# Token shift of the local layers by DMA instead of a matmul, and unit five's up product behind the query and key transposes

## The reference

```
def shift_token(t):                      # half of the channels come from the token before
    t1, t2 = jnp.split(t, 2, axis=-1)
    t2 = jnp.pad(t2, ((0, 0), (1, 0), (0, 0)))[:, :-1]
    return jnp.concatenate([t1, t2], axis=-1)

def _layer(x, wqkv, qs, ksc, wo, lg, lb, w1, b1, w2, b2):
    q, k, v = heads(shift_token(x) @ wqkv)          # 8 heads of 64
    q, k = rotary_xpos(l2norm(q) * qs, l2norm(k) * ksc)
    x = x + local_attention(q, k, v) @ wo           # window 128, causal
    h = shift_token(x)
    h = (h - mean(h)) / sqrt(var(h) + 1e-05) * lg + lb
    a, g = jnp.split(h @ w1 + b1, 2, axis=-1)       # 682 hidden channels each
    return x + (a * gelu(g)) @ w2 + b2
```

## Time and profile before

| | us |
|---|---|
| median of 3 runs | 1770.78 |
| lowest, highest | 1770.05, 1774.5 |
| the profiled execution | 1777.05 |
| its span from the first to the last instruction | 1775.2 |
| phase L1f in the profile | about 486 to 1168 |

### The profile page before, as it was taken

The page is one execution under the profiler, slowest core; times in us unless marked ns, Lnnn a source line. Parts: engine busy times, 40 slices in busy tenths (PEclk is TensorE's granted clock), DMA queues, the critical chain, the costliest instruction groups (busy, mean ns, idle before and its releaser), DMA issues. The chain is left out here.

```text
span 1775.2 us, 38479 instructions
## 1 busy us (share of the span) xinstructions
PE 1678.3 (95%) x11947; PEld 1314.3 (74%) x11992; DVE 1134.9 (64%) x3349; ACT 984.9 (55%) x2789; POOL 936.7 (53%) x1137
## 2 busy tenths in 40 slices
PE   7999799989789999999999999989998999989998
PEld 4788478858646777777777777768876888867886
DVE  4787666638656666766667666547886353336875
ACT  4677345534334566665666656547772355526775
POOL 2366575535456555555555555333677144456752
PEclk9999899999999999999999999999998999999999
DMA  4333276565020000000000000012435244432200
GB/s 156 93 102 119 92 233 196 163 208 180 22 103 1 2 1 1 1 1 1 1 1 1 1 1 1 1 49 83 152 139 184 85 130 143 139 125 76 75 27 25
DMA packets 75574, 138.20 MB, mean 78 GB/s; under 512 B 11697, under 2 KB 57009, under 8 KB 73201
## 3 DMA queue, kind: packets, MB, share of 16 engines
q1 hardware_dynamic: 61648, 96.14, 17.3%
q0 software_dynamic: 13728, 39.60, 6.4%
HBM read 84.88 MB, written 50.82 MB: 76 GB/s over the span
## 5 line engine op out<-in xcount | busy, mean ns | idle before, releaser
L1534 POOL TENSOR_TENSOR L1f_rn<-L1f_ss,L1f_root_c 128x8 f32<-128x8 f32 x64 | 105.6, 1650 | 202.8 <-DVE L1f_ss L1840 200.8
L1667 PE MATMUL L1f_psQ<-L1f_xT,arena 128*128 128x128 f32 x1408 | 167.7, 275 | 0.9 <-ACT L1f_xT L1748 0.9
L1667 PEld LDWEIGHTS L1f_psQ<-L1f_xT,arena 128*128 128x128 f32 x1408 | 164.8, 192 | 2.8 <-ACT L1f_xT L1748 1.1
L2065 POOL DMA_INDIRECT outs_L2f<-L2f_tiles_ys,L2f_tiles_spot x79 | 75.8, 959 | 120.8 <-ACT L2f_tiles_ys L2210 110.5
L1766 ACT ACTIVATE L1f_sg<-L1f_psQ,vec1f 128x128 f32<-128x128 f32 x192 | 63.5, 364 | 118.4 <-PE L1f_psQ L1667 117.6
L1549 POOL TENSOR_TENSOR L1f_rot<-L1f_qn,L1f_sinT 128x512 f32<-128x512 f32 x64 | 113.2, 1788 | 28.8 <-DVE L1f_qn L1856 28.8
L1594 PE MATMUL L1f_psQ<-arena,L1f_hT 128*128 128x512 f32 x256 | 118.4, 605 | 0.6 <-ACT L1f_hT L1755 0.6
L1886 DVE SCALAR_TENSOR_TENSOR L1f_hid<-L1f_psQ,vec1f,L1f_sg 128x128 f32<-128x128 f32 x192 | 61.4, 346 | 78.8 <-ACT L1f_sg L1766 77.7
L2065 POOL DMA_INDIRECT outs_L0f<-L0f_tiles_ys,L0f_tiles_spot x79 | 75.7, 958 | 48.7 <-ACT L0f_tiles_ys L2210 43.0
L1679 PE MATMUL L1f_psB<-arena,L1f_hid 128*128 128x256 f32 (+1 forms) x384 | 99.8, 388 | 0.0
L1539 POOL TENSOR_TENSOR L1f_pr<-L1f_pr,L1f_rs 128x512 f32<-128x512 f32 x64 | 95.6, 1514 | 6.8 <-DVE L1f_rs L1850 6.8
(11 more groups left out here) (534 smaller groups left out, 4682.4 us busy)
## 6 DMA issues: line engine op xcount, KB each, us to landing
L0f_tiles_xs<-rows_L0f SPq DMA_DIRECT2D x79, 144.0 KB, 2.3
L2f_tiles_xs<-rows_L2f SPq DMA_DIRECT2D x79, 144.0 KB, 2.2
arena<-in_w_L2f SPq DMA_DIRECT2D x8, 1120.0 KB, 5.6
arena<-in_w_L1f SPq DMA_DIRECT2D x8, 1088.0 KB, 7.5
L1x_got<-outs_L0f SPq DMA_DIRECT2D x16, 512.0 KB, 3.6
L3x_got<-outs_L2f SPq DMA_DIRECT2D x16, 512.0 KB, 3.4
arena<-in_w_L0f SPq DMA_DIRECT2D x8, 768.0 KB, 4.7
rows_L0f<-zero SPq DMA_DIRECT2D x31, 144.0 KB
```

The costliest lines, as they stand in the source:

```text
L1534: nc.gpsimd.tensor_tensor(rn[:, s.p, h], ss[:, s.p, h], root_c[:, 0:LH], ALU.pow).then_inc(s_rn, 1)
L1667: mm = nc.tensor.matmul(out, w, xT[:, k], start=(k == 0), stop=(k == KC - 1), skip_group_check=True)
L2065: nc.gpsimd.indirect_dma_start(r.outs, bass.IndirectOffsetOnAxis(spot[:, t % YR:t % YR + 1], 0), ys[:, t % YR], None).then_inc(r.s_out[t % ...
```

## The change

The second token shift leaves PE. SP copies partitions 0 to 126 of the upper 128 channels of `Y` to partitions 1 to 127 of a new SBUF tile `ysh`, two buffers by parity of the step; partition 0 keeps the zero of a memset on POOL. DVE waits for the copy on one semaphore per parity and reads `ysh` where it read `psA`. On PE, unit five of `hidden(s, 2)` becomes a piece of its own, `hidden(s, 3)`, behind `turn`. ACT's and DVE's lists keep their order.

```diff
+        ysh = ph.sb("ysh", [P, 2, P])
...
+        s_sh = [ph.sem(f"shifted{i}") for i in range(2)]
...
+            def shift(s):
+                if s.n == 0:
+                    sp.wait_ge(s_one, 4)
+                sp.wait_ge(s_x, s.n + 1)
+                after(sp, s_ln, 2 * s.n - 2)
+                sp.dma_start(ysh[1:P, s.p], Y[0:P - 1, own(s), P:D]).then_inc(s_sh[s.p], 16)
             rounds([(weights_in, 0)])
+            rounds([(shift, -2)])
...
+            nc.gpsimd.memset(ysh[:, :, :], 0.0).then_inc(s_one, 1)
...
             def hidden(s, j):
...
-                for i in range(2):
-                    if j == 2:
+                for i in (0, 1) if j < 2 else (j - 2,):
+                    if j > 1:
                         pe.wait_ge(s_act, U * s.n + 2 + 2 * i)
...
-            def shift(s):
-                pe.wait_ge(s_x, s.n + 1)
-                after(pe, s_xT, s.n)
-                pe.wait_ge(s_hT, min(s.n + 4, N))
-                nc.tensor.matmul(psA[:, 0:P], c.shift, Y[:, own(s), P:D], start=True, stop=True, skip_group_check=True).then_inc(s_sh, 1)
...
-                    (turn_in, 1), (output, -2), (at(hidden, 0), -3), (at(hidden, 1), -3), (at(down, 0), -3), (shift, -2),
-                    (at(hidden, 2), -3), (turn, 0), (at(down, 1), -3), (at(down, 2), -3)])
+                    (turn_in, 1), (output, -2), (at(hidden, 0), -3), (at(hidden, 1), -3), (at(down, 0), -3),
+                    (at(hidden, 2), -3), (turn, 0), (at(hidden, 3), -3), (at(down, 1), -3), (at(down, 2), -3)])
...
             def shifted(s):
-                dve.wait_ge(s_sh, s.n + 1)
-                nc.vector.bn_stats(st[:, s.p, 6:12], psA[:, 0:P]).then_inc(s_st, 1)
+                dve.wait_ge(s_sh[s.p], 16 * (s.n // 2) + 16)
+                nc.vector.bn_stats(st[:, s.p, 6:12], ysh[:, s.p]).then_inc(s_st, 1)
...
-                for k, src in enumerate((Y[:, own(s), 0:P], psA[:, 0:P])):
+                for k, src in enumerate((Y[:, own(s), 0:P], ysh[:, s.p])):
```

More of the change, by code:

```diff
@@ L1489, in local_layers @@
         (s_one, s_mv0, s_root0, s_tab, s_y, s_T, s_hT, s_qk, s_sq, s_ss, s_rn, s_qn, s_cos, s_rot, s_qr, s_qkT, s_qT, s_kT,
-         s_v, s_vx, s_S, s_mx, s_exp, s_rs, s_scaled, s_pt, s_pT0, s_pT1, s_pv, s_oT, s_out, s_x, s_st, s_sh, s_mvf, s_rf,
+         s_v, s_vx, s_S, s_mx, s_exp, s_rs, s_scaled, s_pt, s_pT0, s_pT1, s_pv, s_oT, s_out, s_x, s_st, s_mvf, s_rf,
          s_ln, s_TF, s_xT, s_yb, s_h, s_sg, s_act, s_o, s_res, s_done, s_sm) = ph.semaphores(
             "ones mv0 root0 tab y T hT qk sq ss rn qn cos rot qr qkT qT kT v vx S mx exp rs scaled pt pT0 pT1 pv oT out x "
-            "st shifted mvf rf ln TF xT yb hidden sg act o res done sm")
+            "st mvf rf ln TF xT yb hidden sg act o res done sm")
+        s_sh = [ph.sem(f"shifted{i}") for i in range(2)]
         block = ph.block()
@@ L1515, in _ @@
             nc.gpsimd.memset(spark[:, :], 0.0).then_inc(s_one, 1)
-            pool.wait_ge(s_one, 3)
+            nc.gpsimd.memset(ysh[:, :, :], 0.0).then_inc(s_one, 1)
+            pool.wait_ge(s_one, 4)
             def row_roots(s):
@@ L1651, in turn_in, with unit @@
                 mm.then_inc(s_T, 1)
+            def unit(j, i):
+                return 2 * min(j, 2) + i
             def hidden(s, j):
@@ L1659, in hidden @@
                     after(pe, s_act, U * s.n)
-                for i in range(2):
-                    if j == 2:
+                for i in (0, 1) if j < 2 else (j - 2,):
+                    if j > 1:
                         pe.wait_ge(s_act, U * s.n + 2 + 2 * i)
-                    for m in range(1 if 2 * j + i == U - 1 else 2):
-                        out = unit_out(2 * j + i, m)
+                    for m in range(1 if unit(j, i) == U - 1 else 2):
+                        out = unit_out(unit(j, i), m)
                         for k in range(KC):
-                            w = part(s, UNITS_AT + (2 * j + i) * UNIT_GLU + (m * KC + k) * P, P)
+                            w = part(s, UNITS_AT + unit(j, i) * UNIT_GLU + (m * KC + k) * P, P)
                             mm = nc.tensor.matmul(out, w, xT[:, k], start=(k == 0), stop=(k == KC - 1), skip_group_check=True)
-                    if i == 1 or j == 2:
+                    if i == 1 or j > 1:
                         mm.then_inc(s_h, 1)
```

## The result

| | kernel before | changed kernel |
|---|---|---|
| median, us | 1770.87 (6 runs) | 1762.66 (6 runs) |
| lowest, highest | 1769.8, 1774.5 | 1758.69, 1763.54 |
| span of the profiled execution | 1775.2 | 1760.6 |
| phase L1f in it | 680.94 | 673.76 |
| full round | 20.191 | 19.967 |

The ratio is 0.9948, 95% interval [0.9935, 0.996]: 8.2 us less, where 6.8 were forecast, and the interval reaches from 7.1 to 11.5. The phase's length is from the first to the last start of a PE matmul into its tiles.

A forecast was written before the change was run, and what follows sets the result against it. PE's instruction list was taken to bound full rounds. Removing 31 shifts of 0.22 us gave -6.8 us, the move and copy nothing: 1770.78 - 6.8 = 1764.0 us, own range 1762 to 1766, wider range 1761 to 1774.

The forecast's parts named there:

- What bounds: Full rounds: PE's instruction list sets the length, busy 563.82 of 565.40 us; other engines' waits count only if PE meets them.
- The removed product: Shift matmul on PE: 0.22 us each, 31 of 32 shifts count, 6.8 us less if nothing else gets late.
- The move costs nothing: Unit five behind the transposes: no PE wait becomes late; closest is the key copy, 0.2 us to spare.
- What the move avoids: Unit five in its old place would wait for DVE's products of units two and three, about 0.1 us a round.
- The copy at the high end: SP's copy of 127 partitions, packets one behind another: 4.9 us to land, at no cost to PE.
- The pace of 0.024: Copy on one DMA engine: 0.024 us a packet, from 397 packets in 0.6 us on 16 engines.
- The edge: Copy landing later than 5.5 us after release delays PE at `down`; margin 0.6 us at the high end.
- the late rival: Slower copy packets make `down` wait for DVE's unit four; gain gone from 0.031 us a packet, 1786 us at 0.035; chance 0.16.
- Small parts: Memset of `ysh` on POOL and DVE reading SBUF cost nothing; third round's PE idle grows from 1.01 to over 2 us.
- A second stretch at half clock: Third round, after longer PE idle ahead of the transposes: could cost up to 1.7 us; none taken in the sum.
- More than forecast: Rival: the tail, where hidden layers wait for `normed`, gains a little from earlier statistics; 1762 us, chance 0.04.

The follow-up runs named there:

- e3: Changed kernel without its copy, DVE reading the memset's zeros; full round 19.967 us, ratio to the kernel before 0.9969.
- e4: Changed kernel with the copy split into 112 and 15 partitions; full round 19.967 us, ratio to the kernel before 0.9975.
- e5: Changed kernel with the copy widened to 160, 192 or 256 channels; full rounds 19.967, 20.406, 21.700 us; ratios to the kernel before 0.9968, 1.0061, 1.0426.
- e10: Kernel before with 17 in place of 12 constant matmuls in the third round; third round 20.16 us, ratio to the kernel before 1.0003.
- e11: Changed kernel run once more on another chip; third round 21.55 us, ratio to the kernel before 0.9957.
- e1: Changed kernel with the copy, but unit five back ahead of the transposes; full round 20.146 us, ratio to the kernel before 0.9993.

## Why the prediction was right

- **What bounds.** PE's list sets the round: confirmed by e3 and e4, by e5 with 160 channels, where DVE is 0.9 us late and the round unchanged, and by the same 1.6 us of idle time before and after.
- **The removed product, 0.22 x 31 = 6.8.** Measured 0.224 a round. Of the phase's 7.18 us, 6.28 are the 28 full rounds, 1.83 the third round, of which about 1.6 is the clock, and the tail gives 0.91 back, since its stretch at half clock costs 1.4. The clock's part nearly cancels. The right term is 7.0 (31 x 0.224), as profiles with the stretch in the same place show: e10 against the changed kernel, both in the tail, 680.71 - 673.76 = 6.95, and the kernel before against e11, both in the third round, 680.94 - 674.02 = 6.92. The 0.004 a round above the shift's own time is not located.
- **The move costs nothing.** Right: the key copy ends at 797.59, 0.35 ahead of PE's 797.94, where 0.2 was worked out, because the GELU starts 0.04 after unit five's last matmul ends and not 0.10. Unit five's hidden part is ready at 796.88 for the load at 797.31.
- **What the move avoids, about 0.1 a round.** Undersized: 0.18. That made the second half of the change worth 5 us, as e1's rounds show, and not 3; with this wait most of the gain would have been lost. The sum did not hold this term, so the forecast's number did not test it.
- **The copy at the high end, 4.9 us.** Right in kind, a little long: 4.57, since the first packet and the landing together take 1.5 us. The pace of 0.024 came out right, with some luck: it was read from loads on all engines together, and nothing in that trace showed that one engine copying within SBUF keeps it. The edge is at 5.8 and not 5.5, so the spare time was 1.3 us and not 0.6; by the forecast's own formula the late rival's break-even was nearer 0.034 us a packet than 0.031.
- **Small parts.** The memset took 0.31 us of POOL and moved nothing: the phase's first 54.3 us are the same. A second stretch at half clock, kept for the range, did not come in the changed kernel; the one there was changed its place.
- **More than forecast.** 1762.66 lies nearest this rival's 1762, but not by its mechanism: with the clock alike, the tail gains 39.45 - 39.01 = 0.44 (kernel before and e11), which is two shifts of 0.22 and part of the forecast's 31.
- **The rest.** The measured 8.2 us against the phase's 7.2 is within the intervals (e11's whole ratio is worth 7.8), and nothing shows the 1.0 between them to be the change's; that e3 and e4, with the same rounds, came out at 0.9969 and 0.9975 says how far a median moves by itself. The profiled spans differ by 14.6, of which 7.2 lie in this phase; the other 7.4 lie in phases that the change does not touch. Their stretches at half clock fall differently in every execution, 44.9 us in the profile before and 25.6 in the one after, and 19.3 us less of them can give back up to 9.7. No single pair of profiles should be read for a gain of this size.

## What to carry to other kernels

When one engine is full, taking 0.2 us out of its list is worth that only if every wait behind it has as much to spare. Work out when each wait is met, at the weight load and not at the matmul, and reorder in the same edit: neither half paid alone here (0.045 and 0.000 of 0.224 us a round).

A copy that has 4.6 us of other work to land in may be slow for nothing, but its partition count decides how slow: 127 partitions crossed one behind the other at 21 GB/s and landed in 4.6 us, 112 and 15 apart in 2.5 us.

Judge sub-percent gains by the steady round, which repeated to 0.001 us from chip to chip, while medians of the kernel before moved by 2 to 3% (1769 to 1816). Then look at both ends as well: e5 with 160 channels has the same round and loses 1.1 us in the tail.

## What was not expected of the hardware

- The copy's pace by packet size on one engine, from the widened copies: landings of 4.57, 5.47, 6.28 and 7.54 us for 512, 640, 768 and 1024 bytes, so 640 bytes cost 0.9 us more over 127 packets (0.007 each) where 0.005 was expected from sizes, 768 bytes 1.7 where 1.4 was, and 1024 bytes 3.0 where 2.8 was.
- The 3.4 us at half clock changed places between two executions of the same kernel, third round or tail, 560 us apart. With the copy at 256 channels they came in 11 of 28 full rounds, though PE's idle time ahead of them was only 1.4 to 1.8 us.
- Instruction fetch packets (31 in the full rounds before) never delayed the copy by more than 0.06 us: its landing stayed within 4.56 to 4.62 us in all full rounds.
